# Splitting `up` with a stride of four columns, so that `down` loads in pieces of 4 KB

## The reference

```python
w = weights[conditions]                         # (128, 32, 32)
h = einsum('bct,bcd->bdt', x, w)                # (128, 32, 256) = 4096 tokens of 256
logits = h @ gate_w                             # 8 experts
scale = top_k(logits, 2).sum(-1)
shared = square(relu(h @ up_w)) @ down_w        # 256 -> 1024 -> 256
y = shared + (h @ expert_weight) * scale
out = x + (y - mean(y)) * rsqrt(var(y) + 1e-5) * gamma + beta
```

## Time and profile before

| | |
|---|---|
| time, median of 3 runs | 231.48 us (231.45 to 231.5) |
| the profiled execution, its own time | 231.46 us |
| its span, first to last instruction | 229.8 us |
| TensorE busy | 222.6 us (97%) |
| VectorE / ScalarE / GpSimd busy | 148.3 / 107.4 / 128.8 us |
| DMA moved | 11.81 MB in 16889 packets |

### The profile page before, as it was taken

How to read it: one execution, slowest core, us unless ns; L and a number is a source line. 1 busy time by engine, 2 the same in 40 slices (tenths; PEclk the granted TensorE clock), 3 DMA queues, 4 the chain that set the end, 5 groups by cost and what they waited for, 6 DMA issues and landing times.

```text
span 229.8 us, 4007 instructions
## 1 busy us (share of the span) xinstructions
PE 222.6 (97%) x1266; PEld 191.8 (83%) x1266; DVE 148.3 (65%) x351; ACT 107.4 (47%) x188; POOL 128.8 (56%) x131
## 2 busy tenths in 40 slices
PE   7899999999999999999999999999999999999992
PEld 2697888888888888888888888888888888888992
DVE  6485866666655656765556765556667565566884
ACT  2398945345435544544554554364445345544200
POOL 3729973656546655376536575456653674466511
PEclk9999999999999999999999999999999999999999
DMA  5795303030603020000200002000200002000121
GB/s 186 193 238 148 97 12 101 8 98 7 188 8 98 7 93 2 0 0 3 91 0 3 0 0 94 3 0 0 81 13 0 1 0 96 0 0 0 38 79 68
DMA packets 16889, 11.81 MB, mean 51 GB/s; under 512 B 6628, under 2 KB 16356, under 8 KB 16868
## 3 DMA queue, kind: packets, MB, share of 16 engines
q1 hardware_dynamic: 15140, 9.91, 14.8%
q10 hardware_dynamic: 1312, 1.59, 2.2%
q0 software_dynamic: 416, 0.05, 0.2%
HBM read 7.35 MB, written 4.19 MB: 50 GB/s over the span
## 4 chain that ended last, share of the span: by engine, by line
PE 91%; DVE 2%; DMA 2%; issue 1%; POOL 1%; ACT 1%; POOLq 1%; DVEq 0%
PE up_ps L309 36%; PE down_ps L400 25%; PE down_ps L402 13%; PE hid_ps L282 5%; PE moe_ps L416 3%; PE moe_ps L418 3%; PE moe_ps L417 3%; DMA wd<-in_L_cond_weights_dram 1%; POOL sq_lo L647 1%; POOLq L193 1%; DVE square L522 1%; DVE up_lo L589 1%; DMA cond_row<-in_itok_B_dram 1%; PE down_ps L282 0%; ACT up_hi L466 0%
## 5 line engine op out<-in xcount | busy, mean ns | idle before, releaser
L647 POOL TENSOR_TENSOR sq_lo<-square,sq_hi 128x512 fp32r<-128x512 f32 x64 | 83.8, 1313 | 69.3 <-DVE square L522 68.6
L400 PE MATMUL down_ps<-down_hl,sq_hi 128*128 128x512 f32 x248 | 88.7, 392 | 0.0
L522 DVE SCALAR_TENSOR_TENSOR square<-up_ps,relu 128x512 f32<-128x512 f32 x64 | 44.0, 687 | 41.2 <-ACT relu L460 40.0
L402 PE MATMUL down_ps<-down_hl,sq_lo 128*128 128x256 f32 x248 | 69.6, 280 | 0.0
L400 PEld LDWEIGHTS down_ps<-down_hl,sq_hi 128*128 128x128 f32 x248 | 46.5, 188 | 10.6
L460 ACT ACTIVATE relu<-up_ps 128x512 f32<-128x512 f32 x64 | 38.2, 596 | 32.7 <-PE up_ps L309 32.7
L309 PE MATMUL up_ps<-hid_hi,up_hi 128*128 128x512 f32 (+1 forms) x136 | 53.0, 392 | 0.1
L309 PE MATMUL up_ps<-hid_hi,up_lo 128*128 128x512 f32 (+1 forms) x136 | 51.1, 379 | 0.0
L402 PEld LDWEIGHTS down_ps<-down_hl,sq_lo 128*128 128x128 f32 x248 | 46.7, 188 | 2.4
L462 ACT ACTIVATE sq_hi<-relu 128x512 fp32r<-128x512 f32 x64 | 40.5, 634 | 2.0
L309 PE MATMUL up_ps<-hid_lo,up_hi 128*128 128x512 f32 (+1 forms) x136 | 40.2, 380 | 0.0
(11 more groups left out here) (59 smaller groups left out, 200.7 us busy)
## 6 DMA issues: line engine op xcount, KB each, us to landing
x_sb<-in_x_dram SPq DMA_DIRECT2D x7, 512.0 KB, 3.7
out_dram<-result SPq DMA_DIRECT2D x7, 512.0 KB, 3.1
wd<-in_L_cond_weights_dram SPq DMA_DIRECT2D x110, 4.0 KB, 1.6
result<-in_L_ffn_up_w_dram ACTq DMA_DIRECT2D x2, 512.0 KB, 4.3
x_sb<-in_L_ffn_down_w_dram SPq DMA_DIRECT2D x2, 512.0 KB, 5.6
x_sb<-in_x_dram ACTq DMA_DIRECT2D x1, 512.0 KB, 3.5
out_dram<-result SPq DMA_DIRECT2D x4, 128.0 KB, 1.7
eg_raw<-L_ffn_expert_weight_dram SPq DMA_DIRECT2D x1, 256.0 KB, 3.9
```

The source lines that it names most:

```text
L400: pe.matmul(dst[:, :], a_hi, down_hl[:, c, :, :].rearrange("p s t -> p (s t)"), start=(c == 0), stop=False)
L402: mm = pe.matmul(dst[:, T:2 * T], a_lo, down_hl[:, c, 0, :], start=False, stop=(c == CH - 1))
L522: dve.scalar_tensor_tensor(square[:, c % 2, :], up_ps[c % UPB][:, :], 0.0, relu[:, c % 2, :], ALU.max, ALU.mult).then_inc(square_done, 1)
L647: pool.tensor_tensor(sq_lo[:, j % 2, c, :], square[:, c % 2, :], sq_hi[:, j % 2, c, :].bitcast(f32), ALU.subtract).then_inc(sq_lo_done, 1)
```

## The change

The 1024 intermediate values are renumbered within each half of 512. Chunk `c` (0 to 3) of half `l` was the indices 512 l + 128 c + p; now it is 512 l + 4 p + c, with p from 0 to 127.

For `down` this means that partition p of a load takes the four successive rows 4p to 4p + 3, 4 KB in one piece. For `up` it means that chunk c takes every fourth column of its half, starting at c. `up_raw` is loaded as before; the split reads it with a step of four floats and writes `up_hi` and `up_lo` chunk by chunk without gaps. An instruction now covers one half of the contraction, so that there are `K` = 2 times as many on ScalarE and on VectorE, and the semaphores count accordingly. VectorE's instruction for half k waits for ScalarE's of the same half.

```diff
@@ -42,7 +42,8 @@
     x_rows = x.rearrange("b c t -> (b c) t").rearrange("(g p) t -> p g t", p=P)
     out_rows = out.rearrange("b c t -> (b c) t").rearrange("(g p) t -> p g t", p=P)
     up_rows = up_w.rearrange("(k p) i -> p k i", p=P)
-    down_rows = down_w.rearrange("(c p) h -> p c h", p=P)
+
+    down_rows = down_w.rearrange("(l p c) h -> p l c h", l=DOWN_LOADS, p=P)
 
     ctx = ExitStack()
     with ctx:
@@ -152,6 +153,16 @@
         def split_cols(part):
             return slice(P * UP_SPLITS[part].start, P * UP_SPLITS[part].stop)
 
+
+        def raw_cols(part, k):
+            first, last = UP_SPLITS[part].start, UP_SPLITS[part].stop
+            half = up_raw[:, k, up_cols(first // (CH // UP_LOADS))]
+            chunks = half.rearrange("p (q c) -> p c q", c=CH // UP_LOADS)
+            return chunks[:, first % (CH // UP_LOADS):first % (CH // UP_LOADS) + last - first, :]
+
+        def by_chunk(w, part, k):
+            return w[:, k, split_cols(part)].rearrange("p (c q) -> p c q", q=P)
+
         def down_chunks(part):
             return slice(DOWN_CH * part, DOWN_CH * (part + 1))
 
@@ -220,7 +231,7 @@
             def load_down(load):
                 n = CH // DOWN_LOADS
                 part = slice(n * load, n * (load + 1))
-                sp.dma_start(down_raw[:, part, :], down_rows[:, part, :]).then_inc(down_landed[load], 16)
+                sp.dma_start(down_raw[:, part, :], down_rows[:, load, :, :]).then_inc(down_landed[load], 16)
 
             cond_flat = cond.rearrange("(o b) -> o b", o=1)
             sp.dma_start(cond_row[:, 0:TILES * Q], cond_flat[:, 0:TILES * Q]).then_inc(cond_first_landed, 16)
@@ -312,7 +323,7 @@
             def up_ready(c, ready):
                 for part, chunks in enumerate(UP_SPLITS):
                     if c == chunks.start:
-                        pe.wait_ge(ready, part + 1)
+                        pe.wait_ge(ready, K * (part + 1))
 
 
             def first_rounded(c, half):
@@ -463,8 +474,8 @@
 
             def split_up(part):
                 act.wait_ge(up_landed[part // 2], 16)
-                act.activation(up_hi[:, :, split_cols(part)], up_raw[:, :, split_cols(part)], ACT.Copy) \
-                    .then_inc(up_hi_ready, 1)
+                for k in range(K):
+                    act.activation(by_chunk(up_hi, part, k), raw_cols(part, k), ACT.Copy).then_inc(up_hi_ready, 1)
 
             def split_down(part):
                 act.wait_ge(down_landed[part * DOWN_LOADS // DOWN_PARTS], 16)
@@ -585,9 +596,10 @@
                                          x_sb[:, TILES * j + t, :], ALU.mult, ALU.add).then_inc(result_done, 1)
 
             def split_up(part):
-                dve.wait_ge(up_hi_ready, part + 1)
-                dve.tensor_tensor(up_lo[:, :, split_cols(part)], up_raw[:, :, split_cols(part)],
-                                  up_hi[:, :, split_cols(part)].bitcast(f32), ALU.subtract).then_inc(up_lo_ready, 1)
+                for k in range(K):
+                    dve.wait_ge(up_hi_ready, K * part + k + 1)
+                    dve.tensor_tensor(by_chunk(up_lo, part, k), raw_cols(part, k), by_chunk(up_hi.bitcast(f32), part, k),
+                                      ALU.subtract).then_inc(up_lo_ready, 1)
 
             def split_down(part):
                 dve.wait_ge(down_hi_ready, part + 1)
```

## The result

The changed kernel takes 232.49 us (median of 6 runs, 232.31 to 232.58) against 231.47: a ratio of 1.0043, 95% interval 1.0032 to 1.0053. It is slower by 1.02 us; forecast were 1.14. The profiled execution took 232.45 us, span 230.8.

The account below looks back on a forecast made before the run. TensorE bounds the kernel, its one later stall (0.46 us, `moe`) set by a chain from `square` of chunk 0. Strided splits of `up` add 1.14, other parts nothing: 231.46 + 1.14 = 232.60 us, range 231.2 to 233.0.

Parts of the forecast that it names:

- The bound: TensorE is 97% busy; a later start of `square` of chunk 0 passes whole through `moe` to the end.
- the stall to go: Rival: TensorE's wait for `moe` vanishes, all 0.46 us, giving 231.0; needs `square` of chunk 0 at 15.19; chance 0.03.
- Down in pieces of 4 KB: Load of `down` in longer pieces: credited with nothing, since the relu it feeds is not what `square` waits for.
- The cut: Split of `up` part 2 in two instructions, stride unpriced: better overlap starts `square` of chunk 0 at 15.52, gaining 0.13 us.
- a second turn: Strided `up` splits of 512 cost 0.53 us extra on VectorE, 0.42 on ScalarE; `square` 1.14 later; chance 0.48 (or near it).
- two ends: Bounds on the stride's excess per VectorE subtract of 512 elements: nothing at the lower, 0.78 us at the upper.
- the prediction's chain: Start of `square` of chunk 0 shifts by 2.8 e - 0.34, with excess e on VectorE and 0.8 e on ScalarE.
- the slow rows: `split_down` subtracts of 512 on VectorE beside GpSimd's `add_beta`: 1.04 and 1.46 us instead of 0.68, excess 0.36 and 0.78.
- Parts 0 and 1: Earlier `up` splits: strided copies leave ScalarE free at 8.58, `hid_hi` starts at 8.59, so the cost is just covered.
- TensorE's wait for `moe`: TensorE's stall ahead of 21.01, 0.46 us before the change: forecast above 1 us, ending at 22.15.
- The wait for `eg_lo`: TensorE meets `eg_lo` at 15.99 and waits some 0.3 us, using up part of the longer wait at `moe`.

Follow-up runs that it names:

- the probes: Kernel before plus eight ScalarE copies and eight VectorE subtracts behind its last result, with various steps; 512 elements at read step 4 took 1.11 and 1.06 us.
- the fastest version: Kernel before with the up split cut in dense halves and the second split of `down` moved later on ScalarE and VectorE: 230.94 us against 231.44, ratio 0.9979.

## Why the prediction was right

**The bound.** Right, and shown three ways: with one engine's stride, with the other's, and with both, the start of `square` of chunk 0 and the time move by the same amount; and taking the whole wait away wins 0.50 us, where 0.46 stood in the trace. A later start passes on whole; an earlier one does so only if no link behind it gets longer. With both splits of `down` moved, `square` of chunk 0 came 1.05 us earlier and the time grew, since the split beside `sq_lo` then stood in the chain with 1.48 us. The prediction asked for `square` at 15.19 for the stall to go. It went with 15.30, once the second split of `down` was out of the chain and the first `sq_lo` took 1.29 and not 1.61.

**Down in pieces of 4 KB: nothing.** Right. Alone it moves the time by 0.01 us, and a lead of 0.1 on ScalarE, from a landing as early as both sizes of piece show, ends at VectorE's queue.

**The cut: 0.13 gained.** Right by the profile (`square` at 15.54, a wait of 0.26), and consistent with the time.

**The stride: a second turn.** This was the choice on which the sign hung, between two ends that the trace before could not decide, and that it came out so near is in part luck. It was right in size for the two engines together and a little wrong for each: forecast were 0.42 us extra for a copy and 0.53 for a subtract, measured 0.52 (1.14 to 1.16 for 0.63) and 0.40 (1.09 for 0.69). The prediction took the price of a turn from each engine's own pace; the probes show the same 1.8 ns an element on both. The two errors cancel for the most part: with the measured values the prediction's chain gives 0.52 + 2 x 0.40 - 0.34 = 0.98, against 1.14 forecast and 1.01 measured. The reason given, that it is nearer to the slow rows, was a weak one. A split of `down` is slowed beside GpSimd (1.48 us for 0.68), as those rows are, and with nothing beside it a subtract with a step of two takes 0.69 like a dense one. So those rows don't show that a subtract is without reserve when it reads with a step.

**Parts 0 and 1: just covered.** Nearly. The strided copies leave ScalarE free for `hid_hi` at 8.67 rather than 8.58, 0.08 late on the earlier trace rows. In the same execution TensorE's first conditioning also came 0.16 later, so that it alone would have set nearly that time, and the two can't be told apart here. None of it is left: `split_up(2)` starts at 12.21 in both kernels.

**TensorE's wait for `moe`.** Above 1 us was forecast, 0.63 came. The wait for `eg_lo` was foreseen (0.29 for 0.3), the one for the PSUM bank of chunk 4 was not. Both come out of the longer wait, so the sum does not change. Going by the wait's length alone, one would take 0.17 us for the cost; the later end of `moe` is what counts.

## What to carry to other kernels

When a stall ends in a chain of engines, cost a change by what it does to the start of that chain and to each link in it, not by the length of the stall after it; an earlier start is worth nothing if a link gets longer by as much. If a layout has to put a stride somewhere, compare all places that read it: here a step of 16 bytes cost 0.4 to 0.5 us for each instruction of 512 elements at the start, 13 us in the weight loads, and nothing at the start with a step of 8 bytes. Larger pieces of a transfer are worth nothing while something else holds what waits for it; check that before paying for them.

## What was not expected of the hardware

- The price of a step is the same on two engines and is full from four floats on: 1.06 to 1.12 us for 512 elements with steps 4 and 8, on reads and on writes, against 0.63 and 0.69 with steps 1 and 2 (0.66 for ScalarE's step 2).
- TensorE's weight load of 128 fp32 columns pays for the same step: 313 ns for 188.
- A subtract of VectorE with both inputs in SBUF and one of GpSimd can delay each other, and the one that starts second is delayed: 1.48 us for 0.68 on VectorE, 1.61 for 1.29 on GpSimd. `square`, which has one input in PSUM, took 0.69 beside a `sq_lo` of 1.29 in the fastest version.
